# New orders of work and PSUM slots for all engines, and no identity products, in a two-block vision kernel on one core

## The chip, the cores and the metric

The kernel runs on one core of one Trainium2 chip. The metric is the device time of one execution in microseconds (us); the time before is the median of three runs.

## The reference

`x` has 8 images of 48 channels and 48 x 48 pixels, all in float32. Two blocks follow each other.

```python
# layer 0
qkv = windows(x, 8, 8) @ qkv_w.T + qkv_b                    # 36 windows of 64 tokens, 4 heads of 12
attn = softmax(q @ k.T / sqrt(12) + bias)
x = x + (attn @ v) @ proj_w.T + proj_b
a, b = split(w1 @ x + w1_b)                                  # 1x1, to 2 x 48 channels
g = edge_pad(a * sigmoid(b))
y = conv3x3(g, w2) + w2_b                                    # dense, 48 to 48
x = x + leaky_relu(y, 0.2)
# layer 1
x = x + dwconv(x, cpe1)                                      # depthwise 3x3
y = layernorm(x)
act = silu(act_proj(y)); t = silu(dwconv(in_proj(y), dwc))
q, k = elu(qk(t)) + 1                                        # linear attention, 6 heads of 8
kv = rope(k).T @ t / n; z = 1 / (q @ mean(k) + 1e-6)
y = rope(q) @ kv * z + dwconv(t, lepe)
x = x + out_proj(y * act)
x = x + dwconv(x, cpe2)
x = x + fc2(gelu(fc1(layernorm(x))))
```

## The kernel before

The images are worked on in four pairs `i`, two images side by side in the 128 partitions (48 channels each). Layer 0 works in six strips `n` of 8 rows, layer 1 in three chunks `n` of 16 rows. Pair `i + 1` may be in layer 0 while pair `i` is in layer 1, because most buffers that are kept over a layer (`XP`, `XB`, `LV`) exist twice. `QS`, `QH`, `AR` and `TP` exist once, so the layer-1 work of two pairs follows in turn there.

All order is written by hand, as one list of jobs for each engine: `PE_ORDER` (TensorE), `ACT_ORDER` (ScalarE), `DVE_ORDER` (VectorE), `POOL_ORDER` (GpSimd) and `SP_ORDER` (the DMA queue). A job is `name.i.n`. Each engine runs through its list in order (the loops `for name, i, n in jobs(...)` at the end of each block) and stands at a job until its semaphores are there. In `PE_ORDER`, `@k` is the PSUM slot, of four, that the job fills (`places`, line 208), and `+m` puts m products of the 128 x 128 identity with itself ahead of it in the same slot (`keep_busy`, line 834 on). They compute nothing that is used.

Jobs on TensorE, in the order of one pair:
- layer 0, for a strip: `qk`, `v`, `sc0`/`sc1` (scores, two halves), `tr0`/`tr1` (transposes of the exponentials), `av` (times v), `ot`, `pj` (projection), `w1`. For a chunk: `cv`, the dense 3x3 filter, 36 products.
- layer 1, for a chunk: `d0` (first depthwise filter as 36 products), `xc`, `va` (mean and variance), `ip`, `ac` (two 1x1), `kt`, `vt`, `q`, `kv`; then once for the pair `kp`, `kk` (the matrices from the sums), and for a chunk `dn` (denominators), `at`, `op` (output projection), `d3` (the last depthwise filter), `xc2`, `va2`, `f10`, `f11`, `f12`, `f2`.
- once: `s1`, `s2`, `s3`, products for the biases and weights. `s2` waits for all weights (`loaded_b`).

VectorE: `qb` scales q, `sb0`/`sb1` add the bias and take the maximum, `ob` divides by the sum, `x1` adds the residual, `g` gates. In layer 1: `yn` normalises; `c10` to `c18` are the nine taps of the middle depthwise filter (`dwc`, line 1179) and `c20` to `c28` those of `lepe` (line 1193), all in `scalar_tensor_tensor` on a chunk; `ko`, `qo` finish elu; `ks` sums kv; `kp`, `kk` take the matrices from PSUM; `az`, `am` multiply and merge; `oz`, `yn2`, `o` close the chunk. `z0.0.0` prepares the rotation tables (line 1066) and waits for all weights and tables; `s0`, `s1`, `s2`, `s3` are the other jobs on weights.

ScalarE: `xw`, `kx`, `vx`, `ex` (exponential), `pt`, `oe`, `sg`, `ed`, `yf`, `x3`, `sq`, `rs`, `ie`, `ar`, `ts`, `ke`, `qe`, `ve`, `z`, `x4`, `ge`, copies and functions from PSUM. `table_plan` works out from `ACT_ORDER` where a table of functions has to be loaded. GpSimd: `su0`/`su1` subtract the maximum, `x2` adds the result of layer 0, `kr`, `qs`, `qc` are the rotations of k and q, `ym` multiplies by act. SP: `ld` loads strips of the next pair, `py` and `pz` turn results from one half of the partitions to the other, `st` stores.

The links that the steps of the prediction use: `kp` on VectorE needs TensorE's `kp`, that needs `kv.i.2`; `az` needs `z`, that needs `dn`, that needs `kp` on VectorE; `at` needs `kk`, `qs`, `qc`; `op` needs `ym`, that needs `am`; `oz` needs `op`; `d3.i.0` needs the DMAs `pz.i.0` and `pz.i.1`; `c10` needs `ip` of its chunk and the next; `d0.i.n` needs `x2` of its chunk and the next.

## Time and profile before

| | us |
|---|---|
| median of 3 runs | 836.62 (834.96 to 836.62) |
| the profiled execution | 833.6 |
| its span, first to last instruction | 831.8 |
| TensorE busy with products | 754.8 |
| of these, identity products | 74.0 |
| VectorE busy | 542.9 |
| ScalarE busy | 462.7 |
| GpSimd busy | 305.7 |

Busy times are unions over the span. All matmuls are in float32, and each is recorded as two (a transpose as one), so that 24 jobs of 36 products give 1728 records. In the views, PE is TensorE, PEld its weight loads, DVE VectorE, ACT ScalarE, POOL GpSimd. PEclk is the granted clock of TensorE as a share of 2.4 GHz: 0.5 is 1.2 GHz. L591 is line 591 of the kernel.

### The profile page before, as it was taken

To read this page: it belongs to the slowest core of one execution; us is meant where nothing else is said; L and a number is where in the kernel's file an instruction comes from. 1 tells how busy PE (TensorE), PEld (TensorE's weight loads), DVE (VectorE), ACT (ScalarE), POOL (GpSimd) and SP (SyncE) were. 2 spreads that over 40 slices of the span, in tenths; PEclk is the share of its full clock that TensorE was granted. 3 is DMA by queue.
4 is the path that set the end of the run, shared out by engine and by line. 5 is a ranking of instruction groups with operands and counts; after the bars stand their busy time and mean duration, and the time that the engine had idled before them with its cause. 6 is when DMAs were issued, how large, how long until landed. Compare 5 with 4: busy or idle time off the path is not lost.

```text
span 831.8 us, 19875 instructions
## 1 busy us (share of the span) xinstructions
PE 754.8 (91%) x8514; PEld 477.2 (57%) x8514; DVE 542.9 (65%) x677; ACT 462.8 (56%) x649; POOL 305.7 (37%) x230
## 2 busy tenths in 40 slices
PE   5789999979989999989789999798799998887997
PEld 4678555656754555666544455476464443775654
DVE  3277404999897035899996036999977016889802
ACT  2267347886532477888442487977342459542045
POOL 5133022245862121244971020197822100588200
PEclk9789999999899999899999999999969999989999
DMA  3200030000001220000002110100001100100101
GB/s 58 50 2 3 11 78 1 3 1 2 16 1 31 44 44 2 16 16 15 2 15 37 41 41 2 30 16 1 16 1 30 45 2 16 29 1 1 30 16 44
DMA packets 50505, 16.77 MB, mean 20 GB/s; under 512 B 45584, under 2 KB 50320, under 8 KB 50418
## 3 DMA queue, kind: packets, MB, share of 16 engines
q1 hardware_dynamic: 49906, 15.46, 8.6%
q8 instruction: 68, 1.11, 0.6%
q14 instruction: 19, 0.16, 0.1%
q10 hardware_dynamic: 512, 0.04, 0.0%
HBM read 4.87 MB, written 3.54 MB: 10 GB/s over the span
## 4 chain that ended last, share of the span: by engine, by line
PE 49%; DVE 22%; issue 12%; POOL 8%; SPq 4%; ACT 3%; DMA 1%; DVEq 0%; ACTq 0%; POOLq 0%
PE ps L591 18%; DVE CT L1193 5%; PE ps L682 5%; DVE QS L1179 5%; PE ps L581 5%; PE ps L668 3%; PE ps L838 3%; PE ps L657 3%; SPq L469 2%; POOL KX L1306 2%; PE ps L828 2%; DVE SC L1123 2%; PE ps L766 2%; POOL KX L1299 1%; PE ps L811 1%
## 5 line engine op out<-in xcount | busy, mean ns | idle before, releaser
L1332 POOL TENSOR_TENSOR SC<-SC,mx 128x768 f32<-128x768 f32 x48 | 79.5, 1657 | 225.7 <-DVE mx L1127 225.7
L591 PE MATMUL ps<-XP,wdw 48*64 48x384 f32 x1728 | 143.8, 483 | 0.9 <-ACT QH L1019 0.8
L1193 DVE SCALAR_TENSOR_TENSOR CT<-TP,vec_sb,CT 112x768 f32<-112x768 f32 x96 | 132.7, 1394 | 1.3
L1179 DVE SCALAR_TENSOR_TENSOR QS<-XP,vec_sb,QS 112x768 f32<-112x768 f32 x96 | 111.5, 1186 | 0.6
L591 PEld LDWEIGHTS ps<-XP,wdw 48*64 48x64 f32 x1728 | 66.4, 133 | 71.7 <-issue 64.6
L1024 ACT ACT_TABLE_LOAD x64 | 82.1, 1283 | 1.1
L682 PEld LDWEIGHTS ps<-vx,PT 128*128 128x128 f32 x576 | 70.4, 202 | 13.4 <-issue 6.3
L838 PEld LDWEIGHTS ps<-ident_sb 128*128 128x128 f32 x534 | 67.4, 204 | 18.2 <-issue 13.9
L1165 DVE TENSOR_TENSOR LV<-LV,XB 112x768 f32<-112x768 f32 x24 | 27.3, 1136 | 77.3 <-ACT LV L972 77.3
L682 PE MATMUL ps<-vx,PT 128*128 128x52 f32 x576 | 73.1, 285 | 3.6 <-ACT PT L923 2.4
L838 PE MATMUL ps<-ident_sb 128*128 128x128 f32 x534 | 74.0, 294 | 1.6 <-DVE XB L1251 0.9
L1123 DVE TENSOR_TENSOR SC<-ps,bias_sb 128x768 f32<-128x768 f32 x48 | 45.7, 953 | 45.2 <-PE ps L657 45.1
L591 PE MATMUL ps<-G,w_sb 48*64 48x384 f32 x864 | 73.3, 490 | 0.8 <-ACT G L938 0.7
L903 ACT ACTIVATE kx<-ps,hmask_sb 112x384 f32<-112x384 f32 x96 | 47.8, 584 | 15.1 <-DVE qw L1114 15.0
L1337 POOL TENSOR_TENSOR XP<-XP,YB 112x768 f32<-112x768 f32 x12 | 21.0, 1747 | 92.2 <-DMA YB<-YF 92.2
L591 PEld LDWEIGHTS ps<-G,w_sb 48*64 48x64 f32 x864 | 33.8, 135 | 36.3 <-issue 30.7
L1351 POOL TENSOR_TENSOR CT<-CT,AR 112x768 f32<-112x768 f32 x12 | 21.8, 1815 | 86.5 <-DVE CT L1241 86.5
L923 ACT ACTIVATE PT<-ps 128x768 f32<-128x768 f32 x48 | 38.7, 809 | 25.3 <-PE ps L668 25.1
L919 ACT ACTIVATE SC<-SC 128x768 f32<-128x768 f32 x48 | 40.6, 845 | 16.7 <-POOL SC L1332 16.6
L668 PE MATMUL ps<-ident_sb,SC 128*128 128x128 f32 x288 | 44.3, 296 | 3.9 <-DVE SC L1123 2.8
L657 PE MATMUL ps<-kx,qw 48*64 48x256 f32 (+1 forms) x768 | 43.0, 344 | 4.8 <-ACT kx L903 4.3
L961 ACT ACTIVATE XB<-ps,vec_sb 112x768 f32<-112x768 f32 x12 | 10.8, 901 | 65.5 <-PE ps L591 65.5
(165 smaller groups left out, 1298.4 us busy)
## 6 DMA issues: line engine op xcount, KB each, us to landing
XP<-in_x_dram SPq DMA_DIRECT2D x48, 72.0 KB, 2.4
YB<-YF SPq DMA_DIRECT2D x48, 72.0 KB, 2.2
XP<-XB SPq DMA_DIRECT2D x48, 72.0 KB, 2.3
out_dram<-XB SPq DMA_DIRECT2D x24, 144.0 KB, 2.2
rope_th_sb<-in_rope_th_dram SPq DMA_DIRECT2D x1, 441.0 KB
w_sb<-in_w_dram SPq DMA_DIRECT2D x2, 81.0 KB
wfc_sb<-in_wfc_dram SPq DMA_DIRECT2D x4, 36.0 KB
wln_sb<-in_const_dram SPq DMA_DIRECT2D x6, 9.0 KB
```

The costliest lines, as they stand in the source:

```text
L581: mm = pe.matmul(slot(job)[half(c, HALF), r * BANK:r * BANK + SPX], w[half(r)], src[half(r), c * SPX:(c + 1) * SPX], start=True, stop=True)
L591: mm = pe.matmul(slot(job)[half(c, HALF), r * BANK:r * BANK + SPX], w[half(r), tap * HALF:(tap + 1) * HALF], shifted(t, d * CROWS + c * WI ...
L657: mm = pe.matmul(slot(job)[half(r, HALF), c * BANK + at:c * BANK + at + heads * TOK], qw[n % 2][half(c), w * TOK:(w + 1) * TOK], kx[half(c ...
L668: mm = pe.transpose(slot(job)[:, j * 128:(j + 1) * 128], SC[u % NSC][:, j * 128:(j + 1) * 128], ident_sb[:, :])
L682: mm = pe.matmul(o[:, :, hp * 2 * VCOL:(hp + 1) * 2 * VCOL], PT[t // 3][:, k * 128:(k + 1) * 128], va[:, hp, :, w, :], start=True, stop=True)
L838: pe.matmul(slot(job)[:, 0:128], ident_sb[:, :], ident_sb[:, :], start=True, stop=True)
L903: op_ = act.activation(dst[:, h], src, ACT.Identity, scale=head_mask[h])
L1024: act.preload_act_table_set(TABLE[name, i, n])
L1123: dve.tensor_tensor(sc, two(job, 128).rearrange("p b (j m) -> p b j m", m=TOK), bias_sb[:, :].unsqueeze(1).unsqueeze(1).broadcast_to([128, ...
L1179: dve.scalar_tensor_tensor(out=rows16(T0[n]), in0=win, scalar=wt, in1=rows16(T0[n]), op0=ALU.mult, op1=ALU.add).then_inc(dwc_step, 1)
L1193: dve.scalar_tensor_tensor(out=ct, in0=win, scalar=wt, in1=ct, op0=ALU.mult, op1=ALU.add).then_inc(lepe_step, 1)
L1332: pool.tensor_tensor(sc, sc, bc_last(mx[:, (u % NSC) * 12:(u % NSC) * 12 + 12], TOK), ALU.subtract).then_inc(sub_ready, 1)
```

## The change

All five lists are replaced by others, and with `PE_ORDER` the PSUM slots. No job has a `+m` any more, so none of the 267 identity products is left. The jobs are the same, on the same engines, with the same buffers. `x_loaded` becomes one semaphore for each strip and each of the two `XP` buffers, and its two waits count accordingly, since all `ld.1` now stand ahead of `py.0.0`. In VectorE's list `z0.0.0` moves from the sixth to the sixteenth place. The table plan that follows from `ACT_ORDER` has 53 loads in place of 64.

The diff, cut; of the lists only the passages that are spoken of below stand here.

```diff
 PE_ORDER = """
-    v.0.0@0 v.0.1@1 s1.0.0@2+8 qk.0.0@3 sc0.0.0@0+11 sc1.0.0@1 qk.0.1@2 sc0.0.1@3+12 tr0.0.0@0+4 sc1.0.1@1
-    qk.0.2@2 tr1.0.0@0 av.0.0@0 v.0.2@3 sc0.0.2@2 ot.0.0@0 tr0.0.1@3+4 pj.0.0@1 sc1.0.2@0 qk.0.3@3 tr1.0.1@2
...
-    xc2.2.0@3 d3.2.1@2 va2.2.0@0 d3.2.2@1 f10.2.0@3 xc2.2.1@2 xc2.2.2@0 f12.2.0@1 d0.3.0@3 va2.2.1@2 va2.2.2@0
-    xc.3.0@1 d0.3.1@3 va.3.0@2 d0.3.2@1 xc.3.1@0 ip.3.0@3 xc.3.2@2 va.3.1@1 f11.2.0@0 ac.3.0@3 va.3.2@2
-    ip.3.1@1+3 ac.3.1@2 ip.3.2@0 f2.2.0@1 f10.2.1@3 f12.2.1@0 f11.2.1@2 ac.3.2@1 f2.2.1@3+5 f10.2.2@2 f12.2.2@0
-    f11.2.2@1 f2.2.2@3+5 kt.3.0@2 vt.3.0@1 q.3.0@0 kv.3.0@3+33 kt.3.1@1 vt.3.1@2 q.3.1@0 kt.3.2@3+17 vt.3.2@2
-    q.3.2@1 kv.3.1@0+4 kv.3.2@2+27 kp.3.0@3+6 kk.3.0@0+4 dn.3.0@1 dn.3.1@2 dn.3.2@3 at.3.0@0 at.3.1@1 at.3.2@0
-    op.3.0@2+8 op.3.1@3+6 d3.3.0@1+26 op.3.2@0 xc2.3.0@2+1 va2.3.0@3+4 f10.3.0@1+11 f11.3.0@0 d3.3.1@2 d3.3.2@3
...
+    qk.0.0@0 v.0.0@1 v.0.1@2 s1.0.0@3 sc0.0.0@0 sc1.0.0@1 qk.0.1@3 sc0.0.1@2 tr0.0.0@0 sc1.0.1@1 tr1.0.0@3
+    qk.0.2@0 av.0.0@2 v.0.2@3 sc0.0.2@1 tr1.0.1@0 ot.0.0@2 tr0.0.1@3 sc1.0.2@0 pj.0.0@2 qk.0.3@1 av.0.1@3
+    tr0.0.2@0 v.0.3@2 sc0.0.3@1 s2.0.0@3 tr1.0.2@2 w1.0.0@0 ot.0.1@2 av.0.2@1 pj.0.1@2 v.0.4@3 tr0.0.3@0
...
+    kv.0.1@0 kv.0.2@3 va.1.0@2 kp.0.0@1 kk.0.0@0 dn.0.0@3 at.0.0@1 dn.0.1@0 dn.0.2@2 d0.1.1@3 at.0.1@1 at.0.2@0
+    op.0.0@3 xc.1.1@1 d0.1.2@2 op.0.1@0 va.1.1@1 xc.1.2@3 ip.1.0@2 ac.1.0@0 ip.1.1@1 va.1.2@2 ac.1.1@3 d3.0.0@0
...
+    w1.3.5@1 kt.2.2@2 d0.3.0@0 cv.3.2@3 kv.2.1@1 xc.3.0@2 kv.2.2@0 va.3.0@3 ac.2.1@1 ac.2.2@2 kp.2.0@0 kk.2.0@0
+    dn.2.0@3 dn.2.1@1 at.2.0@0 at.2.1@2 at.2.2@3 dn.2.2@0 d0.3.1@1 op.2.0@2 op.2.1@0 xc.3.1@3 d0.3.2@1 va.3.1@2
+    ip.3.0@0 xc.3.2@3 d3.2.0@1 op.2.2@2 ip.3.1@0 xc2.2.0@3 va.3.2@1 ac.3.0@2 va2.2.0@0 ac.3.1@3 ip.3.2@1
...
 DVE_ORDER = """
-    s1.0.0 qb.0.0 sb0.0.0 qb.0.1 sb1.0.0 z0.0.0 qb.0.2 sb0.0.1 ob.0.0 sb1.0.1 sb0.0.2 x1.0.0 sb1.0.2 qb.0.3
...
+    qb.0.0 s1.0.0 sb0.0.0 qb.0.1 sb1.0.0 s0.0.0 sb0.0.1 sb1.0.1 qb.0.2 ob.0.0 sb0.0.2 sb1.0.2 x1.0.0 qb.0.3
+    ob.0.1 z0.0.0 sb0.0.3 s2.0.0 g.0.0 ob.0.2 x1.0.1 sb1.0.3 x1.0.2 g.0.1 qb.0.4 s3.0.0 g.0.2 sb0.0.4 sb1.0.4
...
+    c27.0.1 c28.0.1 ks.0.1 ks.0.2 kp.0.0 kk.0.0 yn.1.0 az.0.0 am.0.0 az.0.1 am.0.1 az.0.2 oz.0.0 c20.0.2 c21.0.2
...
+    g.3.5 c24.2.0 ko.2.2 c25.2.0 c21.2.1 c26.2.0 c22.2.1 c27.2.0 c23.2.1 c28.2.0 c24.2.1 ks.2.1 c25.2.1 c26.2.1
+    ks.2.2 c27.2.1 kp.2.0 c28.2.1 yn.3.0 kk.2.0 az.2.0 am.2.0 az.2.1 am.2.1 az.2.2 oz.2.0 oz.2.1 c20.2.2 c21.2.2
+    c22.2.2 c23.2.2 c24.2.2 c25.2.2 c26.2.2 c27.2.2 c28.2.2 yn.3.1 am.2.2 oz.2.2 c10.3.0 c11.3.0 c12.3.0 yn.3.2
...
+    ks.3.2 c28.3.1 kp.3.0 kk.3.0 az.3.0 am.3.0 az.3.1 am.3.1 az.3.2 oz.3.0 c20.3.2 c21.3.2 oz.3.1 c22.3.2
...
 POOL_ORDER = """
...
+    su1.3.0 x2.2.2 su0.3.1 su1.3.1 su0.3.2 su1.3.2 su0.3.3 su1.3.3 su0.3.4 su1.3.4 su0.3.5 su1.3.5 x2.3.0 kr.2.0
+    qs.2.0 qc.2.0 x2.3.1 qs.2.1 kr.2.1 kr.2.2 qs.2.2 qc.2.1 qc.2.2 x2.3.2 ym.2.0 ym.2.1 ym.2.2 kr.3.0 kr.3.1
...
 SP_ORDER = """
-    py.0.0 ld.1.0 ld.1.1 py.0.1 ld.1.2 ld.1.3 py.0.2 ld.1.4 ld.1.5 py.1.0 pz.0.0 pz.0.1 pz.0.2 ld.2.0 ld.2.1
...
+    ld.1.0 ld.1.1 ld.1.2 ld.1.3 ld.1.4 ld.1.5 py.0.0 py.0.1 py.0.2 py.1.0 py.1.1 py.1.2 pz.0.0 pz.0.1 pz.0.2
...
-        x_loaded = [sem(f"x_loaded{s}") for s in range(STRIPS)]
+        x_loaded = [[sem(f"x_loaded{j}_{s}") for s in range(STRIPS)] for j in range(2)]
...
-                      .then_inc(x_loaded[s], 16)
+                      .then_inc(x_loaded[i % 2][s], 16)
...
-                    pe.wait_ge(x_loaded[n], i * 32 + 32)
+                    pe.wait_ge(x_loaded[i % 2][n], i // 2 * 32 + 32)
...
-                    act.wait_ge(x_loaded[n], i * 32 + 32)
+                    act.wait_ge(x_loaded[i % 2][n], i // 2 * 32 + 32)
```

## Rows read from the trace of the kernel before

**Rows 1.** The page: the span, busy times, and the chain that ended last.

```profile
span 831.8 us, 19875 instructions
...
PE 754.8 (91%) x8514; PEld 477.2 (57%) x8514; DVE 542.9 (65%) x677; ACT 462.8 (56%) x649; POOL 305.7 (37%) x230
...
PE 49%; DVE 22%; issue 12%; POOL 8%; SPq 4%; ACT 3%; DMA 1%; DVEq 0%; ACTq 0%; POOLq 0%
```

**Rows 2.** Busy time by stretch: from:to, length, each engine, clock, DMA share, GB/s.

```profile
0.00:43.50 43.50, 26.90 (x270) 23.41 (x270) 14.51 (x39) 13.05 (x23) 14.01 (x40) 0.87 0.28 52
43.50:82.80 39.30, 38.97 (x499) 32.90 (x500) 29.40 (x51) 27.22 (x48) 15.09 (x10) 0.92 0.01 2
82.80:648.50 565.70, 525.93 (x6016) 319.50 (x6020) 402.63 (x498) 335.99 (x485) 221.50 (x145) 0.96 0.09 19
648.50:694.30 45.80, 43.09 (x526) 20.01 (x522) 6.19 (x6) 28.61 (x33) 3.38 (x2) 1.00 0.05 13
694.30:758.00 63.70, 54.51 (x547) 42.95 (x539) 55.93 (x53) 31.55 (x33) 38.71 (x27) 0.95 0.06 15
758.00:831.80 73.80, 65.42 (x674) 38.46 (x670) 34.26 (x34) 26.33 (x30) 13.02 (x7) 0.97 0.12 25
```

**Rows 3.** The same stretches, identity products (L838) alone: length, PE, PEld, clock, DMA.

```profile
0.00:43.50 43.50, 12.55 (x70) 11.68 (x70) 0.87 0.28 52
...
82.80:648.50 565.70, 12.62 (x84) 10.51 (x84) 0.96 0.09 19
...
694.30:758.00 63.70, 23.97 (x195) 22.64 (x195) 0.95 0.06 15
758.00:831.80 73.80, 20.91 (x164) 19.01 (x164) 0.97 0.12 25
```

**Rows 4.** Timeline of VectorE: start, duration, line, operation, [idle before <- releaser].

```profile
41.52 0.31 DVE L1069 TENSOR_SCALAR rope_th_sb<-rope_th_sb 98x288 f32<-98x288 f32 x1 [13.96 <-DMA rope_tw_sb<-in_rope_tw_dram]
```

**Rows 5.** Timeline of TensorE at the same time.

```profile
43.54 1.52 PE L645 MATMUL ps<-wv_sb,XW 112*64 112x48 f32 x24 [4.69 <-DVE SC L1123]
```

**Rows 6.** Groups of instructions: line, operation, count | busy, mean ns | idle before.

```profile
L591 PE MATMUL ps<-XP,wdw 48*64 48x384 f32 x1728 | 143.8, 483 | 0.9 <-ACT QH L1019 0.8
L1193 DVE SCALAR_TENSOR_TENSOR CT<-TP,vec_sb,CT 112x768 f32<-112x768 f32 x96 | 132.7, 1394 | 1.3
L1179 DVE SCALAR_TENSOR_TENSOR QS<-XP,vec_sb,QS 112x768 f32<-112x768 f32 x96 | 111.5, 1186 | 0.6
L1024 ACT ACT_TABLE_LOAD x64 | 82.1, 1283 | 1.1
L1332 POOL TENSOR_TENSOR SC<-SC,mx 128x768 f32<-128x768 f32 x48 | 79.5, 1657 | 225.7 <-DVE mx L1127 225.7
...
L1123 DVE TENSOR_TENSOR SC<-ps,bias_sb 128x768 f32<-128x768 f32 x48 | 45.7, 953 | 45.2 <-PE ps L657 45.1
...
L811 PE MATMUL ps<-LV,kv_sb 48*64 48x384 f32 x96 | 12.1, 570 | 2.9 <-DVE kv_sb L1232 1.9 <-DVE QH L1237 0.6 <-ACT YF L949 0.4
```

**Rows 7.** Busy time by stretch, columns as in group 2.

```profile
234.90:406.50 171.60, 160.97 (x1930) 98.97 (x1926) 121.71 (x147) 113.89 (x153) 61.76 (x43) 0.96 0.09 21
```

**Rows 8.** Timeline of VectorE, two runs of seven taps.

```profile
414.41 15.00 DVE L1193 SCALAR_TENSOR_TENSOR CT<-TP,vec_sb,CT 112x768 f32<-112x768 f32 x7
...
777.48 7.33 DVE L1193 SCALAR_TENSOR_TENSOR CT<-TP,vec_sb,CT 112x768 f32<-112x768 f32 x7
```

**Rows 9.** Busy time by stretch around those runs; the last busy time is GpSimd's.

```profile
413.00:427.00 14.00, 12.67 (x127) 6.67 (x127) 13.96 (x11) 7.67 (x10) 13.77 (x7) 0.88 0.06 17
777.50:784.80 7.30, 7.17 (x75) 5.89 (x76) 7.09 (x8) 0.00 (x0) 0.00 (x0) 1.00 0.35 64
```

**Rows 10.** Busy time and granted clock around an idle stretch of TensorE.

```profile
38.80:43.50 4.70, 0.05 (x1) 0.00 (x0) 1.94 (x7) 0.94 (x2) 0.00 (x0) 0.56 0.27 89
43.50:49.60 6.10, 6.06 (x55) 5.31 (x56) 5.92 (x9) 3.64 (x8) 2.94 (x2) 0.50 0.01 3
```

**Rows 11.** Timeline of VectorE after `kp.3.0`.

```profile
764.18 3.42 DVE L1193 SCALAR_TENSOR_TENSOR CT<-TP,vec_sb,CT 112x768 f32<-112x768 f32 x2
```

More of the change, by code:

```diff
@@ new lines @@
+    w1.0.5@1 cv.0.1@3 cv.0.2@0 tr0.1.0@2 sc1.1.0@1 qk.1.1@3 d0.0.0@0 tr1.1.0@2 d0.0.1@1 xc.0.0@3 sc0.1.1@0
+    xc.0.1@2 va.0.0@1 d0.0.2@3 va.0.1@2 sc1.1.1@0 xc.0.2@1 qk.1.2@3 av.1.0@2 va.0.2@1 v.1.2@0 sc0.1.2@3
+    tr0.1.1@2 sc1.1.2@1 qk.1.3@0 ot.1.0@3 ip.0.0@2 pj.1.0@3 tr1.1.1@2 ip.0.1@1 w1.1.0@3 av.1.1@2 tr0.1.2@0
+    sc0.1.3@3 sc1.1.3@1 ot.1.1@2 tr1.1.2@0 pj.1.1@2 qk.1.4@3 v.1.3@0 av.1.2@2 tr0.1.3@0 v.1.4@3 sc0.1.4@1
+    tr1.1.3@0 ot.1.2@2 sc1.1.4@3 qk.1.5@1 pj.1.2@0 av.1.3@2 tr0.1.4@3 v.1.5@0 tr1.1.4@3 ot.1.3@2 ip.0.2@0
@@ new lines @@
+    av.2.5@3 v.3.1@1 f12.1.0@0 f11.1.0@3 f10.1.0@2 cv.2.1@0 ot.2.5@3 qk.3.0@2 f2.1.0@1 f12.1.1@0 f11.1.1@3
+    pj.2.5@2 f10.1.1@1 sc0.3.0@0 sc1.3.0@3 w1.2.5@2 d0.2.0@1 cv.2.2@0 xc.2.0@3 tr1.3.0@2 tr0.3.0@1 qk.3.1@0
+    va.2.0@3 av.3.0@2 sc0.3.1@1 v.3.2@0 sc1.3.1@3 ot.3.0@2 qk.3.2@0 pj.3.0@2 d0.2.1@1 tr0.3.1@2 sc0.3.2@3
+    xc.2.1@0 sc1.3.2@1 tr1.3.1@2 va.2.1@0 ip.2.0@3 av.3.1@2 tr0.3.2@1 v.3.3@0 tr1.3.2@3 ot.3.1@1 qk.3.3@2
+    w1.3.0@0 pj.3.1@3 av.3.2@1 v.3.4@3 sc0.3.3@2 sc1.3.3@0 ot.3.2@3 qk.3.4@1 pj.3.2@3 d0.2.2@2 tr0.3.3@3
@@ L137 @@
[L137 to L140 removed]
+    xw.0.0 xw.0.1 kx.0.0 vx.0.0 vx.0.1 xw.0.2 kx.0.1 ex0.0.0 xw.0.3 ex1.0.0 pt0.0.0 pt1.0.0 ex0.0.1 kx.0.2
@@ new lines @@
+    ed.2.1 z.1.2 ex0.2.3 pt0.2.2 pt1.2.2 kx.2.4 ex1.2.3 pt0.2.3 oe.2.2 vx.2.4 pt1.2.3 ex0.2.4 sg.2.2 kx.2.5
+    ex1.2.4 ed.2.2 x4.1.0 yf.2.0 vx.2.5 pt0.2.4 pt1.2.4 oe.2.3 ex0.2.5 ex1.2.5 x4.1.1 xw.3.0 xw.3.1 x4.1.2
+    pt1.2.5 pt0.2.5 sg.2.3 oe.2.4 ed.2.3 vx.3.0 xw.3.2 sq2.1.0 sq2.1.1 sq2.1.2 sg.2.4 rs2.1.0 rs2.1.1 rs2.1.2
+    ed.2.4 ge2.1.0 ge1.1.0 ge0.1.0 vx.3.1 xw.3.3 yf.2.1 oe.2.5 kx.3.0 ge2.1.1 ge1.1.1 ge0.1.1 sg.2.5 ex0.3.0
+    ed.2.5 ex1.3.0 x3.2.0 yf.2.2 sq.2.0 pt1.3.0 pt0.3.0 kx.3.1 rs.2.0 vx.3.2 xw.3.4 oe.3.0 ex0.3.1 kx.3.2
@@ new lines @@
+    ex1.3.1 x3.2.1 pt0.3.1 sq.2.1 pt1.3.1 rs.2.1 ex0.3.2 ie.2.0 ex1.3.2 pt0.3.2 vx.3.3 pt1.3.2 oe.3.1 xw.3.5
+    kx.3.3 sg.3.0 ed.3.0 vx.3.4 oe.3.2 kx.3.4 ex0.3.3 ex1.3.3 x3.2.2 pt0.3.3 sq.2.2 pt1.3.3 rs.2.2 kx.3.5
+    ex0.3.4 ie.2.1 ex1.3.4 oe.3.3 vx.3.5 pt0.3.4 pt1.3.4 ie.2.2 ex0.3.5 sg.3.1 sg.3.2 ed.3.1 ex1.3.5 sg.3.3
+    ed.3.2 ed.3.3 yf.3.0 pt0.3.5 oe.3.4 pt1.3.5 ts.2.0 ge2.1.2 ge1.1.2 ge0.1.2 ve.2.0 ke.2.0 sg.3.4 oe.3.5
+    ts.2.1 ed.3.4 qe.2.0 ve.2.1 ar.2.0 yf.3.1 ts.2.2 ve.2.2 qe.2.1 qe.2.2 ke.2.1 sg.3.5 ke.2.2 ed.3.5 x3.3.0
@@ new lines @@
+    yf.3.2 sq.3.0 rs.3.0 ar.2.1 ar.2.2 z.2.0 z.2.1 z.2.2 x3.3.1 sq.3.1 x3.3.2 rs.3.1 ie.3.0 sq.3.2 x4.2.0 ie.3.1
+    sq2.2.0 rs.3.2 rs2.2.0 ar.3.0 ar.3.1 ie.3.2 x4.2.1 ge2.2.0 ge1.2.0 ge0.2.0 ts.3.0 x4.2.2 ve.3.0 ke.3.0
+    sq2.2.1 sq2.2.2 ts.3.1 ar.3.2 rs2.2.1 ve.3.1 rs2.2.2 ke.3.1 ts.3.2 ge1.2.1 ve.3.2 ge2.2.1 ge0.2.1 ke.3.2
+    ge2.2.2 ge1.2.2 ge0.2.2 qe.3.0 qe.3.1 qe.3.2 z.3.0 z.3.1 z.3.2 x4.3.0 sq2.3.0 rs2.3.0 ge2.3.0 ge1.3.0 x4.3.1
+    x4.3.2 sq2.3.1 ge0.3.0 sq2.3.2 rs2.3.1 rs2.3.2 ge2.3.1 ge1.3.1 ge0.3.1 ge2.3.2 ge1.3.2 ge0.3.2
```

188 lines of the change are left out of this document (76 added, 112 removed).

## Prediction

> **What bounds the kernel now.** I read the page first. TensorE is busy for 755 of 832 us, VectorE for 543, and the chain that ended last lies on TensorE for 49%, on VectorE for 22% [rows 1]. Then I cut the span into six stretches, at the jobs where the work changes its kind [rows 2]. The reader is to see three regimes there. Up to 43.5 us the inputs arrive. From 43.5 to 648.5 us (the end of `cv.3.2`, the last work of layer 0) TensorE is busy for 565 of 605 us: it is the bound. From 694.3 to 758 us VectorE is busy for 55.9 of 63.7 us and leads (the nine-tap sums of the last image pair, which nothing else can overlap); from 758 us on it is latency, a chain over all engines.
>
> The third view is the identity products [rows 3]. Of their 74.0 us, 12.6 lie in the first stretch, 12.6 between 82.8 and 648.5 us, and 44.9 after 694 us. The last are no work on a bound engine: TensorE would stand there. So 74 us less of TensorE is not 74 us less of time. What I cost is the new order.
>
> **The start.** In the old VectorE order `z0.0.0` stands sixth. It waits for all weights, and VectorE stands behind it for 13.96 us, until 41.5 us [rows 4]; TensorE then starts `v.0.2` at 43.5, after 4.69 us of idle time [rows 5]. In the new order `z0.0.0` stands behind `ob.0.1`, so the second and third strip can go on while the weights arrive. TensorE's `s2.0.0` waits for the same weights, but has 24 us of TensorE work ahead of it, where 13 us were done at 43.5 us before. So at least 11 us of work move ahead of the wait. `s0.0.0`, now sixth, waits only for loads that were issued ahead of those. Bounds 0 and -14; I take **-12**.
>
> **82.8 to 648.5 us.** TensorE's real work there is 525.9 - 12.6 = 513.3 us in 565.7 us, so 1.10 us for each us of work [rows 2, 3]. Ahead of `cv.3.2` the new order no longer has `at.2`, `dn.2` and `op.2` (three each), two `kv.2`, `ac.2.1`, `ac.2.2`, `kp.2.0`, `kk.2.0` and `d3.2.0`; it has `d0.3.0` more. The two convolutions are alike at 143.8 / 24 = 6.0 us [rows 6] and cancel; `at` is 24 us for twelve jobs, 2.0 each (one of its two groups is shown, the other is alike), and the fourteen other jobs are 0.5 to 2.4 us each. That is 17 us, times 1.10: **-18** (0 if these jobs only filled idle time). The 12.6 us of products in this stretch mostly end with the next job starting at once, so it may have been ready sooner: between 0 and -12.6, I take **-10**.
>
> Against it stands a VectorE-bound piece. From `kp.0.0` (234.9 us) to `kp.1.0` (406.5) the old order does 149 us of TensorE work with VectorE busy for 121.7 of 171.6 us [rows 7]. The new one has only 103 us of TensorE work between these two, but all 27 first-filter taps and all 27 second-filter taps of a pair, 27 x 1.19 + 27 x 1.39 = 70 us [rows 6], six bias sums with their maxima (12 x 0.95 = 11 us) and 38 short jobs, together 34 us: 115 us of VectorE. There is a place, too, where it stands: `kk.0.0` and `az.0.0` follow `kp.0.0` almost at once, where the old order had six taps to do; I allow 13 us for the waits of this piece. So 128 us where 103 x 1.12 = 115 would be: **+13**, bounds 0 and +30.
>
> `cv.3.2` then ends at 648.5 - 12 - 18 - 10 + 13 = 621.5 us, and VectorE's `g.3.5`, which stood 11 us ahead of it and now stands 14, comes at 607.5 us (637.4 before).
>
> **The tail.** The new VectorE order has 46.8 us of work from `g.3.5` to `oz.2.2`, which was nearly all done before: 22 second-filter taps at 1.39 are 31 us [rows 6], and sixteen short ones make 16. GpSimd has nearly all its layer-1 work of pair 2 at the same time, which for one pair is (305.7 - 14.0 - 79.5) / 4 = 53 us [rows 1, 2, 6]. Such a tap costs 15.00 / 7 = 2.1 us at 414 us, where GpSimd is busy for 13.8 of 14 us, and 7.33 / 7 = 1.05 us at 777 us where it is idle [rows 8, 9]. With 1.85 in place of 1.39 that is +10 (0 to +16). A tap grows by about 1.1 us beside GpSimd. The Trainium skill (SBUF — State Buffer, Who interferes with whom) says that a VectorE instruction with two SBUF inputs contends for one exclusive port pair with a GpSimd instruction that reads SBUF. By that rule the bias sum, one of whose inputs lies in PSUM, would be spared; its mean over all 48, many of them beside GpSimd, is 953 ns [rows 6], and the trace agrees. If the pair were handed over only after a whole GpSimd instruction each time, the sum would be 12 us more.
>
> Two waits stand in that queue: `kk.2.0`, `az.2.0` behind `kp.2.0`, and `oz.2.2` right behind `am.2.2`, which needs GpSimd's `ym.2.2` and TensorE's `op.2.2`, and `op.2.2` now stands behind the convolution `d3.2.0`. I take 8 us for both (5 to 20). So `oz.2.2` is at 607.5 + 47 + 10 + 8 = 672.5 us; before, the first tap of pair 3 began at 694.3.
>
> From there to `kp.3.0` the old order took 63.7 us [rows 2]. The new one has four more taps ahead of it (5.9 us) and four normalising products (4.5): 74 us, to 746.5. From `kp.3.0` on the old one took 73.8 us. The four taps that moved stood between `kp.3.0` and `az.3.1` as filling (two of them took 3.4 us [rows 11]) while VectorE had to wait for the denominators anyway, so only 1 of the 5.9 us comes back: 73.
>
> **The clock.** With no products TensorE is idle more often here, and a stretch early on shows what follows: after an idle 4.7 us the clock is at 0.50 (1.2 GHz) for the next 6.1 us, though TensorE is busy throughout [rows 10]. The old tail has 0.95 and 0.97 in its last two stretches [rows 2], so it has little of this. For six or seven such returns at 0.5 to 1 us each on the path I take **+5** (0 to +25). Eleven table loads fewer on ScalarE (53 for 64, at 1.28 us [rows 6]) take 14 us off an engine that is busy for 463 us: 0 to -5, I take -3.
>
> The separate semaphores for the two buffers' loads, the PSUM slots and the order of the DMA issues cost nothing: the early `ld.1` only stand behind the weights, with the first use over 50 us later; if they did delay `py.0.0`, it would be by the 12 issues, under 5 us.
>
> **Sum.** 746.5 + 73 + 5 - 3 = 821.5 us of span. The profiled execution took 833.6 us for a span of 831.8, and the median of the runs, 836.6, is 3 us above it. So 821.5 + 1.8 + 3 = **826 us**.
>
> **The rivals.**
> *A, better filled, 805 us.* The VectorE piece costs nothing beside TensorE (-13) and the two waits in the tail are filled (-8). For it: VectorE is idle for over a quarter of 82.8 to 648.5 us. Against: both queues run in order, and the taps need the engine that also does the softmax. Chance 0.17.
> *B, given back, 836 us.* The start and the middle gain as said, but the tail takes 10 us more: `oz.2.2` holds all taps of pair 3 while `op.2.2` waits behind `d3.2.0`, which waits for `ym.2.1`, `op.2.1` and a DMA. It decides where that wait passes 15 us. Chance 0.15, of it 0.05 faster, 0.08 the same, 0.02 slower.
> *C, the clock, 846 us: slower.* The tail's products were what held the clock at 0.95. Without them the sparse work of the last 130 us stays at 1.2 GHz. Of TensorE's jobs on the last chain some 25 us would double (three convolutions at 6.0, then the short ones): +25 for the +5 in the sum. It turns the sign where it costs over 16 us, with the granted clock under about 0.7 after `kp.3.0`. For it: [rows 10]. Against: convolutions of 6 us bring the clock back by themselves. The Trainium skill (TensorE: Matmul & The Clock Gate, What's actually happening) says that the throttled state is the default and activity lifts it; by that rule taking the products out is a loss wherever TensorE's next job lies on the path, which is this rival. The stretch early on agrees with the rule [rows 10], and no row tells how much of the tail would be hit. Chance 0.15.
> *D, queues that stand, 848 us: slower.* One mechanism again: VectorE, in order, stands at `az` behind `kk` in pairs 0, 1 and 2, and TensorE with it, 8 us more each time than I allow. It decides from 11 us in all. For it: in those pairs the new order has two or three jobs between `kp` and `az`, the old one has eight in pair 0. Against: TensorE has convolutions queued there. Chance 0.13.
>
> **How the numbers follow.** My case has 0.40; 0.17, 0.15, 0.15 and 0.13 are the rivals'. A measurement of this kernel tells about 0.2% from no change. Faster: 0.40 + 0.17 + 0.05 = 0.62. The same: 0.08. Slower: 0.02 + 0.15 + 0.13 = 0.30. The range for 8 in 10 goes from 798 (below A by its share of the start's and the products' bounds) to 850 (C and D). Within my case alone it is 815 to 837.
>
> **What would show it.** The first step: no VectorE wait of 14 us ends at 41 us, and `cv.0.2` ends near 103 (115 before). The second: `cv.3.2` ends near 621, with the VectorE piece from `kp.0.0` to `kp.1.0` at 128 us. The third: first tap of pair 3 near 672, and mean taps of 1.85 us before it. The clock: 0.85 or more after `kp.3.0`; under 0.7 C is right. I would be wrong above all if `cv.3.2` ends after 640, that is if TensorE's 1.10 doesn't hold in the new order.

## The result, and the profile after

The changed kernel takes 799.24 us (797.81 to 804.51) beside 836.62 us for the kernel before (834.96 to 839.40): a ratio of 0.956, 95% interval 0.951 to 0.961. It is 4.4% faster. I had forecast 826 us, so the direction held and the size was less than a third of what came. Ratios leave out runs far above the fastest of their kernel, among them one of e1's ten (1374.8 us) and two of e15's four (850 us). The span is 797.9 us where it was 831.8 [rows 1]. The page of the changed kernel, span, busy times and the chain that ended last:

```profile
span 797.9 us, 18796 instructions
...
PE 700.2 (88%) x7980; PEld 416.0 (52%) x7980; DVE 533.2 (67%) x677; ACT 450.3 (56%) x638; POOL 309.1 (39%) x230
...
PE 58%; DVE 19%; issue 7%; POOL 6%; ACT 5%; SPq 4%; DMA 1%; ACTq 0%; DVEq 0%; POOLq 0%
```

The 267 products are 534 matmul records of 74 us [rows 3]; TensorE's busy time fell by 54.6 us only, since some of the work that is left now runs at the lower clock. To see where the time went I cut the changed kernel at the same jobs as the old one. The busy times by stretch (from:to, length, TensorE, weight loads, VectorE, ScalarE, GpSimd, granted clock, DMA share, GB/s):

```profile
104.50:244.40 139.90, 128.60 (x1490) 81.48 (x1490) 102.24 (x126) 77.68 (x117) 62.44 (x40) 0.95 0.04 10
244.40:365.40 121.00, 107.20 (x1300) 60.74 (x1300) 102.36 (x112) 84.44 (x109) 56.23 (x40) 0.94 0.11 24
365.40:470.80 105.40, 100.62 (x1206) 58.37 (x1210) 53.81 (x79) 60.59 (x93) 32.55 (x20) 1.00 0.13 27
470.80:589.70 118.90, 115.31 (x1354) 73.28 (x1346) 93.95 (x119) 78.99 (x116) 49.98 (x31) 1.00 0.05 14
589.70:646.80 57.10, 47.40 (x498) 24.01 (x498) 34.23 (x34) 22.41 (x26) 24.97 (x17) 0.79 0.08 17
646.80:712.40 65.60, 52.03 (x572) 31.17 (x568) 59.11 (x60) 44.87 (x48) 28.73 (x21) 0.87 0.08 19
712.40:797.90 85.50, 59.56 (x510) 23.23 (x506) 29.87 (x30) 26.89 (x30) 21.60 (x13) 0.72 0.10 22
```

The cuts are the ends of the jobs `cv.0.2` (104.5), `kp.0.0`, `kp.1.0`, `cv.2.2`, `cv.3.2` (589.7), the first tap of pair 3 (646.8) and `kp.3.0` (712.4). Against the kernel before:

| stretch | before | after | difference | forecast |
|---|---|---|---|---|
| start to `cv.0.2` | 115.0 | 104.5 | -10.5 | -12 |
| `cv.0.2` to `cv.3.2` | 533.5 | 485.2 | -48.3 | -15 |
| `cv.3.2` to the end | 183.3 | 208.2 | +24.9 | +17 |

The start is read from one trace each, and it varies: in the ten traces here of kernels with the whole start of the changed one (after, e4, e6, e9 to e11, e13, e15 to e17) `cv.0.2` ends at 104.5 to 111.0 us, with a median of 106.4. A difference of two us there says nothing; lengths from `cv.0.2` on are the safer ones.

So the question of this study is the middle row. The whole of it, after, in the columns of above:

```profile
104.50:589.70 485.20, 451.72 (x5346) 273.87 (x5346) 352.37 (x435) 301.70 (x433) 201.20 (x129) 0.97 0.08 18
```

In it TensorE is idle for 485.2 - 451.7 = 33.5 us (39.7 before). From 365.4 to 589.7 it is busy for 215.9 of 224.3 us at a clock of 1.00. What still makes it wait is short. The longest waits of TensorE from 104.5 to 589.7 us, changed kernel (total, times, longest):

```profile
PE ps L579 <- DVE G L1158: 5.7, 1, 5.7
PE ps L787 <- DVE kv_sb L1223: 4.2, 2, 3.5
PE ps L589 <- issue: 3.2, 1, 3.2
PE ps L764 <- issue: 2.4, 2, 1.3
```

### The profile page after: what moved, and what is told of

It reads as the page before. It is cut to its first block, busy times and chain, and to the rows that moved or that the text cites. A ratio compares the mean times of both kernels' runs of the same rounds, so it can differ in the third digit from the quotient of the medians.

```text
span 797.9 us, 18796 instructions
## 1 busy us (share of the span) xinstructions
PE 700.2 (88%) x7980; PEld 416.0 (52%) x7980; DVE 533.2 (67%) x677; ACT 450.3 (56%) x638; POOL 309.1 (39%) x230
## 4 chain that ended last, share of the span: by engine, by line
PE 58%; DVE 19%; issue 7%; POOL 6%; ACT 5%; SPq 4%; DMA 1%; ACTq 0%; DVEq 0%; POOLq 0%
PE ps L589 25%; PE ps L579 8%; DVE QS L1177 6%; PE ps L680 5%; DVE CT L1191 4%; PE ps L666 3%; PE ps L655 3%; PE ps L809 3%; PE ps L764 2%; SPq L467 2%; PE ps L826 2%; DVE SC L1121 1%; DVE LV L1163 1%; PE ps L634 1%; PE ps L643 1%
## 5 line engine op out<-in xcount | busy, mean ns | idle before, releaser
L589 PE MATMUL ps<-XP,wdw 48*64 48x384 f32 x1728 | 152.7, 506 | 9.6 <-issue 9.6
L1191 DVE SCALAR_TENSOR_TENSOR CT<-TP,vec_sb,CT 112x768 f32<-112x768 f32 x96 | 122.8, 1295 | 1.3
L589 PEld LDWEIGHTS ps<-XP,wdw 48*64 48x64 f32 x1728 | 69.7, 140 | 88.4 <-issue 83.7
L1177 DVE SCALAR_TENSOR_TENSOR QS<-XP,vec_sb,QS 112x768 f32<-112x768 f32 x96 | 104.5, 1130 | 0.5
L680 PEld LDWEIGHTS ps<-vx,PT 128*128 128x128 f32 x576 | 66.3, 192 | 9.1 <-issue 6.1
L680 PE MATMUL ps<-vx,PT 128*128 128x52 f32 x576 | 68.5, 275 | 0.6 <-ACT PT L921 0.3
L1297 POOL TENSOR_TENSOR KX<-KX,rope_th_sb 98x384 f32<-98x384 f32 x12 | 18.6, 1550 | 86.5 <-DVE KX L1198 86.5
L655 PE MATMUL ps<-kx,qw 48*64 48x256 f32 (+1 forms) x768 | 43.1, 351 | 7.5 <-ACT kx L901 7.4
L1125 DVE TENSOR_REDUCE mx<-SC 128x12 f32<-128x768 f32 x48 | 45.8, 953 | 1.7
L666 PE MATMUL ps<-ident_sb,SC 128*128 128x128 f32 x288 | 42.5, 288 | 4.7 <-ACT SC L917 1.9
L666 PEld LDWEIGHTS ps<-ident_sb,SC 128*128 128x128 f32 x288 | 32.9, 147 | 17.0 <-issue 10.6
L764 PE MATMUL ps<-KX,VT 98*64 98x144 f32 x384 | 30.0, 315 | 11.5 <-issue 6.9
```

The costliest lines, as they stand in the source:

```text
L589: mm = pe.matmul(slot(job)[half(c, HALF), r * BANK:r * BANK + SPX], w[half(r), tap * HALF:(tap + 1) * HALF], shifted(t, d * CROWS + c * WI ...
L655: mm = pe.matmul(slot(job)[half(r, HALF), c * BANK + at:c * BANK + at + heads * TOK], qw[n % 2][half(c), w * TOK:(w + 1) * TOK], kx[half(c ...
L666: mm = pe.transpose(slot(job)[:, j * 128:(j + 1) * 128], SC[u % NSC][:, j * 128:(j + 1) * 128], ident_sb[:, :])
L680: mm = pe.matmul(o[:, :, hp * 2 * VCOL:(hp + 1) * 2 * VCOL], PT[t // 3][:, k * 128:(k + 1) * 128], va[:, hp, :, w, :], start=True, stop=True)
L764: mm = pe.matmul(slot(job)[half(b, HALF), 0:3 * C], VT[kc % 2][:, t, b, :], KX[kc % 2][:, t, b].rearrange("p m c -> p (m c)"), start=(t == ...
L1177: dve.scalar_tensor_tensor(out=rows16(T0[n]), in0=win, scalar=wt, in1=rows16(T0[n]), op0=ALU.mult, op1=ALU.add).then_inc(dwc_step, 1)
```

## Experiments: the products

**e1, the old kernel without any product.**

```diff
-    v.0.0@0 v.0.1@1 s1.0.0@2+8 qk.0.0@3 sc0.0.0@0+11 sc1.0.0@1 qk.0.1@2 sc0.0.1@3+12 tr0.0.0@0+4 sc1.0.1@1
+    v.0.0@0 v.0.1@1 s1.0.0@2 qk.0.0@3 sc0.0.0@0 sc1.0.0@1 qk.0.1@2 sc0.0.1@3 tr0.0.0@0 sc1.0.1@1
...
```

> The old kernel with all 267 identity products taken out and nothing else changed. My theory: of the 74 us of products most stood in idle time; those between 82.8 and 648.5 us (12.6 us) partly held the next job up, so cv.3.2 ends 5 to 11 us earlier, and the tail loses 5 to 12 us to a lower clock: 826 to 838 us in all. Rival 1 (the products were what cost the time): the whole gain comes from here, 800 to 810 us. Rival 2 (the products held the clock everywhere): over 850 us.

839.6 us, ratio 1.0042 (1.0009 to 1.0076): slower by 0.4%. `cv.3.2` ends at 648.0 (648.5 with them), and from `kp.3.0` to the end it takes 78.3 us (73.8). I had expected 826 to 838 us and `cv.3.2` 5 to 11 us earlier. So taking the products out is no part of the gain; in the middle they cost nothing, and I had counted -10 there. In the tail, where TensorE would stand idle, they were worth 4.5 us: without them the clock there is 0.80, with them 0.97 [rows 2]. The middle and the tail of e1:

```profile
114.00:648.00 534.00, 486.08 (x5620) 294.04 (x5620) 393.16 (x468) 325.62 (x463) 219.26 (x144) 0.95 0.09 19
...
757.30:835.60 78.30, 52.91 (x506) 20.57 (x506) 34.12 (x34) 26.44 (x30) 12.77 (x7) 0.80 0.11 24
```

(`cv.0.2` ends at 113.3 in e1, so the middle is 534.7 us long.)

Since e1 has no products either, it is the fair partner of the changed kernel. TensorE is idle for 47.9 us in it, 14.4 more than after. I also added up TensorE's jobs of the middle, each with the median time that its like takes at full clock: an estimate, 456 us in e1 and 438 us after. Busy time beyond that is what jobs took over it at the low clock: 487 - 456 = 31 us in e1 and 452 - 438 = 14 us after. The clock track of the traces agrees: in the middle it stands at the lower level for 58 us in e1 and for 27 us after, and half of each would be lost by work that goes on. So the 49 us between the two are some 18 us of jobs that now stand behind `cv.3.2` or ahead of `cv.0.2`, 14 us of idle time, and some 17 us of half-speed work.

**e4, the changed kernel with 268 products put back into its tail** (in front of twelve jobs that wait, much as the old one had them).

```diff
-    ... q.3.0@3 q.3.1@2 kv.3.2@1 q.3.2@0 kp.3.0@3 kk.3.0@2 dn.3.0@0
+    ... q.3.0@3 q.3.1@2 kv.3.2@1 q.3.2@0 kp.3.0@3+36 kk.3.0@2+34 dn.3.0@0
...
```

> The new kernel with 268 identity products put back, all in the last 200 us, ahead of the jobs before which TensorE stood (kv.2.2, kk.2.0, kv.3.0, kp.3.0, kk.3.0, at.3.2, d3.3.0, va2.3.0, three f12 and f2 jobs). Theory of the clock: in the new tail TensorE's work took 23 us longer than the same work at full clock, some half of it on the path; with the products it falls by 8 to 14 us, to 785 to 791 us. Rival: what is slow there isn't on the path, or the products hold the next job up as much as they help: 797 to 803 us.

801.07 us, ratio 0.958 (0.951 to 0.965): the same as without, where I had expected 785 to 791. The busy times from `kp.3.0` on in e4:

```profile
714.30:799.30 85.00, 78.18 (x806) 52.27 (x806) 27.78 (x29) 26.47 (x30) 18.20 (x11) 1.00 0.10 22
```

The clock is 1.00 in place of 0.72, and the stretch is 85.0 in place of 85.5 us. Where the clock's gain goes shows at the first of the three convolutions there, `d3.3.0`, first after, then in e4:

```profile
741.43 8.70 PE L589 MATMUL ps<-XP,wdw 48*64 48x384 f32 x72 [6.34 <-issue]
...
750.91 1.02 DVE L1243 SCALAR_TENSOR_TENSOR XB<-ps,vec_sb,XB 112x768 f32<-112x768 f32 x1 [5.66 <-PE ps L579]
```
```profile
745.01 6.04 PE L589 MATMUL ps<-XP,wdw 48*64 48x384 f32 x72
...
751.84 1.02 DVE L1243 SCALAR_TENSOR_TENSOR XB<-ps,vec_sb,XB 112x768 f32<-112x768 f32 x1 [8.25 <-PE ps L579]
```

At full clock it takes 2.7 us less. But the products in front of it let it begin later. It needs eight DMAs of `pz.3.0` and `pz.3.1`. The last lands at 741.3 us after, and `d3.3.0` starts at 741.4; in e4 it lands at 740.3, and `d3.3.0` starts at 745.0, since the products ahead of it run from 733.65 to 745.1. Up to these DMAs e4 was ahead: their first is issued 140.6 us after `cv.3.2` in e4, 144.7 without products. So the higher clock gave 4 us and then 2.7, and the 4.7 us for which the products hold up `d3.3.0` take most of it back; VectorE's next step (`oz.3.2`) comes 37.5 us after `kp.3.0`, 38.5 without them. e4 shows what these 268 products are worth, nothing; it does not show that the low clock is free. My rival C (846 us) is false: its mark, a clock of about 0.7 after `kp.3.0`, was there, and its price of 25 us was not. The Trainium skill (TensorE: Matmul & The Clock Gate, What's actually happening) has the throttled state as the default that activity lifts; the two clocks, 0.72 and 1.00, agree with that. What I had drawn from it, a loss where the next job is on the path, e1 shows at 4.5 us in its tail.

## Experiments: the start

**e2, the old kernel with `z0.0.0` behind `ob.0.1`; e3, the changed kernel with `z0.0.0` sixth.**

```diff
-    s1.0.0 qb.0.0 sb0.0.0 qb.0.1 sb1.0.0 z0.0.0 qb.0.2 sb0.0.1 ob.0.0 ... s0.0.0 ob.0.1 sb0.0.3
+    s1.0.0 qb.0.0 sb0.0.0 qb.0.1 sb1.0.0 qb.0.2 sb0.0.1 ob.0.0 ... s0.0.0 ob.0.1 z0.0.0 sb0.0.3
```

> The old kernel with one job moved in VectorE's list: z0.0.0 from the sixth place to behind ob.0.1, as in the new kernel. My theory: VectorE no longer stands for 14 us at the weights, and cv.0.2 ends 8 to 12 us earlier; 825 to 829 us. Rival: TensorE's own list waits for the same weights soon after, and the rest of the start is latency: under 4 us, 833 us or more.

> The new kernel with z0.0.0 put back to the sixth place, behind sb1.0.0. If the start is worth the same in both kernels: 10 to 12 us more, 809 to 811 us. If the new order has slack after the start (a wait behind it that ends late anyway): under 5 us more.

e2: ratio 0.9935 (0.9894 to 0.9976), `cv.0.2` at 109.9, five earlier where I had expected 8 to 12. e3: 819.6 us, ratio 0.979 (0.973 to 0.985), 20 us over the changed kernel, with `cv.0.2` at 121.3 (104.5) and `cv.3.2` 19 us late. So one place in a list is worth 5 us in one kernel and 20 in the other. `z0.0.0` in the changed kernel, then in e3 (line 1034, since the list is shorter by lines there):

```profile
42.46 0.31 DVE L1067 TENSOR_SCALAR rope_th_sb<-rope_th_sb 98x288 f32<-98x288 f32 x1 [2.55 <-DMA rope_tw_sb<-in_rope_tw_dram]
```
```profile
41.15 0.31 DVE L1034 TENSOR_SCALAR rope_th_sb<-rope_th_sb 98x288 f32<-98x288 f32 x1 [21.37 <-DMA rope_tw_sb<-in_rope_tw_dram]
```

The wait ends at about the same time in all of them (41.2 to 42.5 us); the wait is 21 us in e3 and 14 us in the old kernel because the new order gets to it sooner. It gets there sooner by a second edit that I had missed. TensorE's first scores, in the kernel before and after:

```profile
21.61 2.21 PE L657 MATMUL ps<-kx,qw 48*64 48x256 f32 x32 [2.97 <-ACT kx L903]
```
```profile
13.19 2.84 PE L655 MATMUL ps<-kx,qw 48*64 48x256 f32 x32 [2.11 <-ACT kx L901]
```

In the old ScalarE order `kx.0.0` stands behind `xw.0.3`, which waits for the fourth strip of the image; in the new one it stands third, and TensorE's `qk.0.0` is first.

**e12, the old kernel with both edits**, `qk.0.0` first on TensorE and `qb.0.0` first on VectorE (products ahead of 60 us out as well). **e8, the same with `z0.0.0` alone moved**, and the same products out. The ScalarE part of e12:

```diff
-    xw.0.1 xw.0.2 vx.0.0 xw.0.3 vx.0.1 kx.0.0 kx.0.1 ex0.0.0 ex1.0.0
+    xw.0.1 kx.0.0 vx.0.0 vx.0.1 xw.0.2 kx.0.1 ex0.0.0 xw.0.3 ex1.0.0
```

> The old kernel with the start of the new one as far as its lists allow: z0.0.0 behind ob.0.1, no products ahead of 60 us, ScalarE's kx.0.0 ahead of xw.0.2 and xw.0.3 (which wait for later strips of x), qk.0.0 first on TensorE and qb.0.0 first on VectorE. In the new kernel the first scores start at 13 us, in the old one at 21.6, since kx.0.0 stood behind xw.0.3. Theory: the missing half of the start's gain was this second wait, and cv.0.2 ends near 100 us (107 with the late z0 alone and no products, 115 before); 823 to 829 us if the rest of the old order hands it on. Rival: strip 1 is then held by something else, and cv.0.2 stays at 106 or later.

> The old kernel with z0.0.0 behind ob.0.1, as in the run before with that name, and with no identity products ahead of 60 us (those of s1, sc0.0.0, sc0.0.1, tr0.0.0, tr0.0.1, av.0.1). The late z0 alone gave 5 us here and 20 us in the new kernel. Theory (the products ahead of sc0.0.1, 4.9 us, and the old order of strip 1 took the place of the wait): 3 to 6 us more are won, 823 to 827 us. Rival (what held strip 1 is ScalarE and VectorE, and the products filled idle time): within 2 us of 829.7.

e12: 826.97 us, ratio 0.988 (0.983 to 0.994), `cv.0.2` at 105.7 and `cv.3.2` at 636.6: the start is worth 9 us at the one, 12 at the other and 10 (5 to 14) at the end, and it is kept. I had hoped for `cv.0.2` near 100; it stands where the changed kernels have it. e8: ratio 0.9988 (0.9956 to 1.002), though `cv.0.2` came at 107.1. There `kp.1.0` ended at 401.6 and `cv.3.2` at 645.0, so of the eight microseconds five were left at the first and three and a half at the second, and none that can be measured at the end (I had expected 823 to 827 us). Why e8 loses its gain and e12 keeps it I can't say; e8's ten runs lie between 826.5 and 838.4 us, and one of them is traced.

## Experiments: what sets the middle

My theory after e1 was that VectorE had slack in both kernels and that the old order lost its time in single badly placed waits. The rival was that VectorE's load sets the pace.

**e5, the old kernel with light taps**: the last four taps of both nine-tap filters (`c15` to `c18`, `c25` to `c28`) of pairs 0 to 2 work on one row of sixteen, so the output lacks most of them. **e13, the same in the changed kernel.**

```diff
-                    win = shifted(XP[i % 2], n * CROWS, CROWS, TAPS[k])[0:RG]
+                    rr = 1 if (i < 3 and k >= 5) else CROWS; win = shifted(XP[i % 2], n * CROWS, CROWS, TAPS[k])[0:RG]
...
-                        dve.scalar_tensor_tensor(out=rows16(T0[n]), in0=win, scalar=wt, in1=rows16(T0[n]),
+                        dve.scalar_tensor_tensor(out=rows16(T0[n])[:, 0:rr], in0=win[:, 0:rr], scalar=wt, in1=rows16(T0[n])[:, 0:rr],
```

> The old kernel with less work on VectorE before the last pair: in pairs 0 to 2 the last four taps of both nine-tap filters (c15 to c18, c25 to c28) work on one row of sixteen, so the sums of these pairs lack most of these taps; every job, its place and its waits stay. That is 8 x 9 = 72 taps less, some 75 us of VectorE's 453 ahead of g.3.5. Theory (TensorE's loss between cv.0.2 and cv.3.2, 60 us for 474 us of work, is set by VectorE's load): cv.3.2 ends 20 to 35 us earlier, near 615 to 628 us. Rival (the loss comes from how the jobs follow each other in the lists, whatever VectorE's load): cv.3.2 ends less than 10 us earlier.

> The new kernel with the taps from the fifth on of pairs 0 to 2 made on one row instead of all of theirs, so the output lacks them; everything else as it is. In the old order the same edit moved cv.3.2 from 648.5 to 631.0 us (17.5 us), of which some 13 us were idle time taken away. Theory, the new order leaves TensorE hardly anything to wait for from 365 to 590 us (8.4 us of idle time in six gaps), so VectorE's taps cost it little there: cv.3.2 comes 0 to 8 us earlier than 589.7, so at 582 to 590, and most of that before 365 us. Rival, VectorE's load sets the pace in the new order too (as the loss of 36 us for 36 us of added work suggests): cv.3.2 comes at least 15 us earlier, at 575 or before.

e5 took 821.9 us in its one run and e13 769.9. From `cv.0.2` to `cv.3.2`, e5 and then the two halves of e13, cut at `kp.1.0`:

```profile
115.00:631.00 516.00, 489.49 (x5710) 302.85 (x5706) 335.76 (x468) 325.89 (x463) 198.16 (x144) 0.96 0.09 19
```
```profile
106.50:351.90 245.40, 228.69 (x2794) 141.74 (x2790) 168.73 (x238) 161.54 (x225) 109.20 (x80) 0.98 0.08 17
351.90:574.60 222.70, 216.46 (x2561) 132.53 (x2560) 135.79 (x199) 139.30 (x210) 77.52 (x54) 0.99 0.09 20
```

VectorE has 57 us less to do in e5 and 48 us less in e13, and the stretch is 17.5 and 17.1 us shorter: 0.31 and 0.36 us for each. For e5 I had expected 20 to 35 us by the theory of VectorE's load and under 10 by the other. By its number the rival, that VectorE's load sets the pace, wins in e13 (`cv.3.2` at 574.6, the bound was 575), but the place is as the theory had it: 15.5 of the 17.1 us come before `kp.1.0` (260.9 to 245.4), and 1.6 us from there on (224.3 to 222.7), where TensorE had no idle time to give.

**e6, the changed kernel with 48 unused maxima of 743 ns on VectorE ahead of the `x1` sums of pairs 2 and 3 (35.7 us if added up; as they overlap a little, they cover 32.7). e14, the same in the old kernel. e11, the same 48 in the changed kernel, but ahead of the taps `c10` to `c17` of pair 2.**

```diff
-                    wait_filled(dve, job)
+                    wait_filled(dve, job); [dve.tensor_reduce(junk[:, (ks - 12) * 4 + u:(ks - 12) * 4 + u + 1], w2_sb[:, :], AX.X, ALU.max) for u in range(4 if i >= 2 else 0)]
```

> The new kernel with work added on VectorE that nobody uses: four maxima over w2 (112 x 576, estimated 0.75 us each by the 0.95 us of 768 columns) ahead of each residual sum x1 of pairs 2 and 3, 48 in all, some 36 us, between 370 and 580 us, where VectorE has only 141 us of work for 220 us of TensorE's. Theory of the load: VectorE stays under its limit (177 of 220 us), but the rate of TensorE falls from 1.02 towards the 1.13 of the old kernel: 10 to 20 us more. Rival: there is slack, and under 5 us are lost.

> The old kernel with the 48 unused maxima (0.74 us each on VectorE, 35.7 us in all) ahead of the x1 sums of pairs 2 and 3, at the same jobs as in the new kernel, where they moved cv.3.2 by 35.5 us and the end by about as much. Theory, the old order loses its time to how jobs wait for each other, and so VectorE has slack between them: cv.3.2 moves by 10 to 25 us, and the kernel takes 850 to 862. Rival, VectorE's load sets the pace in the old order just as in the new one: cv.3.2 moves by 33 to 40 us, and the kernel takes 870 to 877.

> The new kernel with the same 48 unused maxima on VectorE (0.74 us each, 35.7 us in all) in another place: two ahead of each of the first eight taps of the middle filter of pair 2 (c10 to c17, three chunks), and no longer four ahead of each x1 of pairs 2 and 3. Ahead of x1 they cost 34 us. Theory of the place (x1 is what TensorE's next jobs wait for, the taps are not): under 15 us more, 799 to 814 us. Rival (VectorE's total in that stretch sets the pace): again 30 us or more, 829 us and above.

e6: 832.97 us, 34 over the changed kernel, where I had expected 10 to 20 (ratio 0.9964, 0.9926 to 1.0003), `cv.3.2` at 625.2, 35.5 us later. e11: 833.3 us (0.9958, 0.9920 to 0.9995), `cv.3.2` at 620.8, 31.1 later. e14: 877.4 us (1.0505, 1.0466 to 1.0544), `cv.3.2` at 691.6, 43.1 later. From 104.5 to `cv.3.2` in e6, and from 114.6 in e14:

```profile
104.50:625.20 520.70, 471.95 (x5364) 283.05 (x5356) 380.46 (x482) 301.80 (x433) 199.35 (x131) 0.93 0.07 17
```
```profile
114.60:691.60 577.00, 521.72 (x5715) 322.68 (x5710) 419.03 (x516) 326.26 (x463) 216.91 (x144) 0.90 0.08 17
```

VectorE is busy for 73% of both stretches, and yet a microsecond more on it costs 0.9 to 1.2. In e6 TensorE is idle for 48.7 us (33.5 without the maxima) and busy for 19 us more with the same jobs (`cv.0.2` ends at 105.7 in e6; from there it is 470.8 for 451.7): a gap that makes it wait also makes its next jobs slow, and the clock is 0.93 where it was 0.97. So my theory of slack falls.

How much of the change is the rival, VectorE's load? The instructions are the same on both pages (677), but not in the middle: there VectorE is busy for 352.4 us after and for 393.2 in e1, mainly because second-filter taps of pair 2 now stand behind `cv.3.2`. At the price of a microsecond taken off (0.31 in e5) these 41 us are worth 13 us, at the price of one added 36 or more. e5 speaks for the lower one: with 335.8 us on VectorE, 17 less than after, the old order's middle is still 516.3 us long, 31 us more than after. Put at the load of after it would be 36 more. So of the 49 us some 18 are TensorE's moved jobs, some 13 VectorE's lower load, and some 18 are left, all estimates. In these 18 are the work taken off ScalarE (301.7 us for 325.6 in e1), the places in the lists and the PSUM slots; no run parts them.

**e7, one bad place mended in the old kernel**: `x1.3.3` three taps earlier, because TensorE waits 5.3 us for it, its longest wait in that stretch.

```diff
-    c20.2.1 c27.2.0 c21.2.1 c28.2.0 x1.3.3 c22.2.1
+    c20.2.1 x1.3.3 c27.2.0 c21.2.1 c28.2.0 c22.2.1
```

> The old kernel with one job moved in VectorE's list: x1.3.3 stands ahead of c27.2.0, c21.2.1 and c28.2.0, and no longer behind them. TensorE stood for 5.3 us at 596 us, because kk.2.0 fills the PSUM slot that x1.3.3 reads. Theory of the gaps (a gap costs its length and then the half-speed clock after it): the gap goes, and cv.3.2 ends 6 to 9 us earlier; 827 to 831 us. Rival (VectorE's queue only moves the wait to the next job): under 3 us.

837.05 us, ratio 1.0001 (0.9973 to 1.0030). The wait before (in e1 as in the old kernel), and what stands in e7 where it was:

```profile
PE ps L789 <- DVE XP L1153: 5.3, 1, 5.3
```
```profile
602.71 5.33 PE L648 MATMUL ps<-vx,PT 128*128 128x52 f32 x24 [4.59 <-DVE SC L1089]
```

The wait moved to `av.3.4`, whose 24 matmuls then take 5.33 us, where 24 of the same line take 2.88 at full clock. `cv.3.2` still comes 2.4 us earlier (646.1), but `kp.3.0` 2.7 later (760.7), so nothing is left at the end, where I had expected 6 to 9 us. A single wait taken away was not time won here.

**e10, e6 with 144 products ahead of the twelve jobs that wait most in it.**

```diff
-    qk.2.3@2 ot.2.1@0 w1.2.0@1 pj.2.1@0 kp.1.0@3 sc0.2.3@2 w1.2.1@0 kk.1.0@1
+    qk.2.3@2 ot.2.1@0+10 w1.2.0@1 pj.2.1@0 kp.1.0@3 sc0.2.3@2 w1.2.1@0+12 kk.1.0@1
...
```

> The new kernel with the 48 unused maxima on VectorE of the run before (833.0 us) and with 144 identity products ahead of the twelve jobs before which TensorE then stood. Theory (half of those 34 us is the half-speed clock after the gaps, not the gaps): 8 to 14 us come back, 819 to 825 us. Rival (the slow products aren't what the chain waits for): within 3 us of 833.

850.85 us, ratio 1.017 (1.013 to 1.021), 18 us over e6, where I had expected 8 to 14 us less than e6. The products alone from 104.5 to `cv.3.2` in e10 (length, TensorE, weight loads, clock):

```profile
104.50:643.90 539.40, 41.16 (x288) 38.77 (x288) 0.95 0.07 17
```

Of their 41.2 us, 18 show in the length from `cv.0.2` to `cv.3.2` (537.4 for 519.5). The rest covers idle time (41.6 us for 48.8) or comes back as clock (16 us by the full-clock sum, an estimate). So products did not let this order run dense; in this stretch, where TensorE has work queued, they cost a little under half of their own length.

**e15, the changed kernel with two more table loads ahead of each of the 29 planned ones of pairs 1 and 2.** Of these 58 the trace has 51.

```diff
-                    act.preload_act_table_set(TABLE[name, i, n])
+                    [act.preload_act_table_set(t) for t in (("gelu_and_others", "exp_and_others", TABLE[name, i, n]) if 0 < i < 3 else (TABLE[name, i, n],))]
```

> The new kernel with two more table loads ahead of each planned one of pairs 1 and 2: 29 loads are planned there, so 58 more at 1.28 us, some 74 us more on ScalarE. Theory, table loads lie on the path of those jobs that TensorE waits for, and the 11 loads that the new order saves are worth a part of the 48 us: the kernel takes 15 to 45 us more, 814 to 845, so that one load is worth 0.3 to 0.8 us, and the 11 saved 3 to 8. Rival A, ScalarE's time is never the pace: within 5 us of the new kernel, 797 to 804. Rival B, ScalarE is the pace throughout: 65 us or more, 865 and over, and the 11 saved loads are worth their full 14 us.

```profile
L1022 ACT ACT_TABLE_LOAD x104 | 133.4, 1283 | 1.2
```

Ratio 1.0001 (0.9947 to 1.0054) where the changed kernel has 0.956: 0.044 x 835 = 37 us for 133.4 - 68.0 = 65 us of ScalarE, 0.6 for each. That is 0.7 us a load, in the middle of what the theory allowed. All four runs lie from 834.2 to 850.4 us, so the cost may be as high as 51; the trace is of a long one (849.99), and its middle is 42.7 us longer for 50 us of loads. If the loads that the new order saves lie no better or worse than these, the eleven are worth about 8 us, an estimate (I had taken 3).

The prices then stand side by side: 0.9 to 1.2 us for each one added on VectorE, 0.6 to 0.8 on ScalarE, 0.45 for products on TensorE, 0.3 to 0.4 for each one taken off VectorE. As I read it, no engine bounds the middle alone: the jobs of one strip run through all four, every queue is in order, and PSUM has four slots, so a delay on one engine is passed on by the next. After, fewer of these meet: TensorE has 16 gaps over 0.5 us in the middle where e1 has 32. Which neighbours in which list bring that, how much of it comes from the lower load alone, and what the new PSUM slots do, is not shown: no run here has one list or the slots of one kernel in the other.

## Experiments: the tail

**e16, the changed kernel with another GpSimd order (e9 is the same kernel, run earlier); e17, the changed kernel beside it.**

```diff
-    qs.2.0 qc.2.0 x2.3.1 qs.2.1 kr.2.1 kr.2.2 qs.2.2 qc.2.1 qc.2.2 x2.3.2 ym.2.0 ...
-    kr.3.2 qs.3.0 qs.3.1 qs.3.2 qc.3.0 qc.3.1 qc.3.2 ym.3.0 ym.3.1 ym.3.2
+    qs.2.0 qc.2.0 x2.3.1 kr.2.1 kr.2.2 qs.2.1 qc.2.1 qs.2.2 qc.2.2 x2.3.2 ym.2.0 ...
+    kr.3.2 qs.3.0 qc.3.0 qs.3.1 qc.3.1 qs.3.2 qc.3.2 ym.3.0 ym.3.1 ym.3.2
```

> The new kernel with GpSimd's list changed in two places: kr.2.1, kr.2.2 ahead of qs.2.1 (TensorE stood 4.4 us at kv.2.2), and for pair 3 qs and qc of one chunk after the other instead of all qs and then all qc. If GpSimd sets the pace of the tail: 3 to 7 us less, 792 to 796 us. If VectorE's queue does: within 2 us of 799.2.

> The new kernel with GpSimd's qs and qc of pair 3 each behind its own q (and kr.2.1, kr.2.2 ahead of qs.2.1), now on the same chip as the new kernel itself, e17. The profiles gave spans of 792.9 and 797.9 us, but the ratios to the old kernel were both 0.956. Theory: kp.3.0 comes about 5 us earlier and the end with it, so 2 to 6 us less than e17. Rival: the 5 us are given back before the end, within 2 us of e17.

> The new kernel unchanged, for comparison with e16 on the same chip. 797 to 801 us.

e9: 796.75 us, ratio 0.956 (0.950 to 0.962). e16: 797.1 us, ratio 0.954 (0.951 to 0.958); e17, on the same chip: 804.3 us, ratio 0.961 (0.957 to 0.965). I had expected 2 to 6 us less than e17. So this version beats the old kernel, and the changed one by 7 us in this pair; e9 and the changed kernel, run at different times, had the same ratio, so the gain is not settled. What the traces show is not what I made it for. From `kp.3.0` to `at.3.2` it takes 19.5 us in both. From `cv.3.2` to `op.2.2` it takes 48.0 us in e16 and 50.8 in e9, but 54.9 in e17 and 54.7 in the changed kernel's first profile. So the traces gain at pair 2's part of the edit, `kr.2.1` and `kr.2.2` first, not at pair 3's; no run has either part alone. In the changed kernel TensorE's `kv.2.2` waits for `kr.2.2`, which stands behind `qs.2.1`, and then GpSimd's `qc.2.1` waits for `ac.2.1`, which stands behind `kv.2.2`: each queue holds up the other. In e16 TensorE's wait is 1.74 us, and GpSimd runs from 584.2 to 618.2 us without one. The two waits in the changed kernel:

```profile
597.24 4.11 PE L764 MATMUL ps<-KX,VT 98*64 98x144 f32 x32 [4.35 <-issue]
...
604.29 1.47 POOL L1315 TENSOR_TENSOR LV<-QH,rope_y_sb 112x768 f32<-112x768 f32 x1 [3.84 <-PE ps L579]
```

## Why the forecast was right or wrong, step by step

**The start** (-12): -10.5, and `cv.0.2` at 104.5 for the forecast 103 (the median of ten traces is 106.4, which makes it -9), with some 3.5 us more of work ahead of it than I had counted (`qk.1.0`, `v.1.0`, `v.1.1`, `sc0.1.0`). The wait of 14 us is gone as I said. But the step named one cause of two: `z0.0.0` alone gives 5 us in the old kernel (e2), and only with `kx.0.0` ahead of `xw.0.3` some 10 us (e12).

**Jobs moved behind `cv.3.2`** (-18): right in the sum. At full clock these jobs are some 14.5 us where I had 17 (an `at` is 1.3 to 1.5 us, not 2.0), and the four now ahead of `cv.0.2` are 3.5 more.

**The products in the middle** (-10): wrong, it is 0 (e1). I had written that the next job "may have been ready sooner"; it was not, or was slower without them. Without this term my forecast would have been 836 us, the old time.

**The VectorE piece** (+13): mis-sized. From `kp.0.0` to `kp.1.0` it took 121.0 us, not 128. That is still TensorE's slackest piece, 13.8 us idle; of the 15.5 us that e13 gains ahead of `kp.1.0`, 5.3 fall in it and 10.2 ahead of it. VectorE is busy for 102 us in it, not 115. A part of that is the taps, which take 1.13 and 1.30 us in the changed kernel where I had the old one's 1.19 and 1.39 [rows 6]:

```profile
L1191 DVE SCALAR_TENSOR_TENSOR CT<-TP,vec_sb,CT 112x768 f32<-112x768 f32 x96 | 122.8, 1295 | 1.3
...
L1177 DVE SCALAR_TENSOR_TENSOR QS<-XP,vec_sb,QS 112x768 f32<-112x768 f32 x96 | 104.5, 1130 | 0.5
```

**The rate of 1.10.** This is the step that failed: the sum let all work that stays in the middle keep its old pace, and so put the change of pace at nothing. I took 1.10 us for each us of TensorE's work as a property of the kernel, and said that I'd be wrong "if TensorE's 1.10 doesn't hold in the new order"; I looked for that on one side only. In its own terms, time over busy time, it is 534.7 / 486.8 = 1.10 in e1 and 485.2 / 451.7 = 1.07 after. That is the smaller half, since the busy time itself holds the half-speed work. Over the jobs' full-clock time it is 534.7 / 456 = 1.173 in e1 and 485.2 / 438 = 1.108 after. The difference on 438 us is some 28 us, most of the 33 us by which the middle was shorter than forecast (485.2 for 518.5). What brought the better pace is in part less load on VectorE and ScalarE in the middle, in part open. The reason I gave for rival A, VectorE idle for over a quarter, was half right: e6 and e14 show that idle VectorE time is no slack.

**The tail** (+17): +24.9, close by terms that don't hold. `g.3.5` to `oz.2.2` took 67.1 us for the forecast 65. But in it VectorE is busy for 44.8 and idle for 22.3 us; I had 57 and 8. The 21 taps L1191 there have a mean of 1.35 us, not 1.85. One tap beside GpSimd and eight without it:

```profile
609.15 2.62 DVE L1191 SCALAR_TENSOR_TENSOR CT<-TP,vec_sb,CT 112x768 f32<-112x768 f32 x1
...
631.43 8.40 DVE L1191 SCALAR_TENSOR_TENSOR CT<-TP,vec_sb,CT 112x768 f32<-112x768 f32 x8
```

Nine of the 21 run where GpSimd is idle and take 1.02 us. The twelve beside it take 1.6 us on average, not the 2.1 of [rows 8]. For the bias sum the mean stays at 953 ns, as [rows 6] had it. From the first tap of pair 3 to `kp.3.0` it took 65.6 us for 74: mis-sized, with VectorE busy for 59.1 us. From `kp.3.0` to the end it took 85.5 us for 75. I counted what moved on VectorE and forgot GpSimd. The stretch holds two losses, GpSimd's and the clock's. GpSimd's `qs` and `qc` of pair 3 wait for `q.3.0`, which shares a buffer with `f2.2.2` (702.4 us), and run up to 729 us in the changed kernel:

```profile
706.57 1.47 POOL L1315 TENSOR_TENSOR QS<-QH,rope_y_sb 112x768 f32<-112x768 f32 x1 [3.31 <-DVE QH L1204]
...
726.60 2.40 POOL L1317 TENSOR_TENSOR LV<-LV,rope_x_sb 112x768 f32<-112x768 f32 x1
```

so `at.3.2` ends 19.5 us after `kp.3.0`, where the old kernel took 12.4.

**The clock** (+5): about right as far as is known. It is 4.5 us in e1's tail, where the clock is 0.80. In the new tail e4 leaves it open: the full clock gave some 7 us up to the end of `d3.3.0`, an estimate from the 4.1 and 2.7 above, and the products took most of it back. **Table loads** (-3): about -8, an estimate (e15). **Luck.** The gain in pace (28 us) was in part hidden in the total by the products' term, which never came (+10), and by a tail 8 us longer than forecast. **The rivals.** A, 805 us, was nearest, but only the first of its two reasons came, and that in half: the VectorE piece cost 6 us and not 13, while VectorE's waits in the tail grew. B's tail did take 8 us more, but not at its place: `oz.2.2` waited 3.0 us, and came 67.1 us after `g.3.5`. C is refuted by the time and by e1's price of 4.5 us. D didn't come: TensorE waited for `kv_sb` 4.2 us in two times in the whole middle.

## What to carry to other kernels

The ratio of time to work on the bound engine belonged to one order of work here: where the order is new, give it a range of its own, to both sides, before any edit is costed, and count how the other engines' load moves over the cut too. An engine's idle share was no slack here, where jobs pass through several in-order queues; one added or removed load on each engine (e6, e13, e15) prices them in a way that no view of the profile does. When fillers are put back to see what a clock is worth, look at when the job behind them could have started (e4). And look for every wait that ends before the one you found: `z0.0.0` was worth 5 us or 20, by what stood around it.

## What the hardware showed that I had not expected

A granted clock of 0.80 in place of 0.97 over the last 78 us cost 4.5 us (e1), and raising it from 0.72 to 1.00 with 268 products won nothing, as they held up the job behind them by 4.7 us (e4). In the middle the low clock costs too: in e6, 15 us more of idle time came with 19 us more of busy time for the same jobs. And two VectorE loads with the same total, at different places (e6, e11), moved `cv.3.2` by 35.5 and 31.1 us: the place mattered little.
